# Feed-forward weights summed and rounded in chunks during the attention loop, and a feed-forward block two tiles deep

## The chip, the cores and the metric

The kernel runs on one core of one Trainium2 chip. The time is that of one execution on the device in microseconds (us), the median of several runs. PE is TensorE, DVE VectorE, ACT ScalarE, POOL GpSimd, SP SyncE, whose queue issues all DMAs here.

## What is computed

Two gated residual blocks over x (32 batches of 100 rows, 512 wide) and a context (32 batches of 361 rows, 256 wide):

```
xn = layernorm(x)
q = rmsnorm(xn @ Wq) * gq ; k = rmsnorm(ctx @ Wk) * gk ; v = ctx @ Wv     (16 heads of 128)
x = x + tanh(g_xattn) * (softmax(q k^T / sqrt(128)) @ v) @ Wo

weight_quant(w): s = max(mean(|w|), 1e-5);  clip(round(w / s), -1, 1) * s
act_quant(x):    r = 127 / max(|x| of the row);  round(x * r) / r
bitlinear(x, w) = act_quant(x) @ weight_quant(w)^T
h = layernorm(x)
x = x + tanh(g_ffn) * bitlinear(silu(bitlinear(h, Wgate)) * bitlinear(h, Wup), Wdown)
```

Wgate and Wup are 2048x512, Wdown is 512x2048. Before the products each of the three becomes a matrix of -1, 0 and 1 and one scale, which needs the mean over the whole matrix first.

## The kernel before

**Two blocks, one after the other.** `attention_block` writes x after attention to DRAM (`x1_rows`), 3200 rows. `ffn_block` reads them back in 25 tiles of 128 rows. All DMAs of the first are done before the second begins.

**Attention.** The 32 batches are handled as 16 pairs (`PAIRS`). A pair has 8 units (`UNITS`), a unit being one batch and one group of 4 heads; units are written in twos (`two_turns(i, u, last, par)` with u = 1, 3, 5, 7 and v = u + 1). Matrix factors in fp32 are split into a high and a low bf16 part and multiplied with three matmuls (`product`, lines 23 to 25). Within a unit PE makes keys for unit u+2 (three tiles of up to 128 context rows), scores for unit u+1, and mixes of probabilities and context for unit u. Keys pass through the other engines in a chain: ACT squares them (L554), DVE sums the squares (`sum_keys`, L737), POOL turns the sum into a scale with two small operations (`key_scale`, L986 and L989), DVE scales (`scale_keys`, L747, writes `khat`), ACT takes the high half (L549), POOL the low half (`keys_lo`, L995, a subtract of two 128x512 inputs), and SP turns both with a DMA transpose. POOL also computes the query scale (`query_scale`, L1001) from `qvar` (DVE, L821) and splits the next pair's context into `nat` (`split_ctx`, L1025 and L1027). On DVE `row_max` (L755), `row_bias` (L765, writes `nbias`) and `probs_lo` (L777) serve the softmax.

Every engine has its own in-order list, written out by hand; semaphores tie them together. Two key banks alternate (`keys_ps`), so the keys of tile n wait for `khat` of tile n-2; two shared banks (`shared_ps`) go round queries, squares, mixes and head outputs, and each use waits until DVE has freed the use before last (`shared_free`). Fourteen pairs run in a hardware loop of 7 turns (`BODY` = 2 pairs a turn, `LOOPS` = 7), the last two are written out.

**Feed-forward.** The block loads the three weight matrices (4 MB each) into SBUF, sums absolute values on ACT (`abs_sums`, L1341, four pieces of 128x2048 a matrix), adds over partitions with a matmul (L1266), divides, clips and rounds on DVE (`ternary`, L1477 and L1479), turns every 128x128 piece on PE (L1280) and casts it on ACT (L1353). Only then does the first `gate_up` start. Per tile:

- DVE: statistics (`x_stats`, L1396 and L1399), `x_quant` (L1404 to L1418), `hidden` (L1426 and L1429, four pieces of 512), `hidden_quant` with a pass over 128x2048 (L1441), `residual` (L1448).
- POOL: `deviation`, two small operations (L1243, L1245).
- PE: `gate_up`, 32 matmuls of 512 columns (L1300), the turning of x (L1290), `down`, 16 matmuls (L1308).
- ACT: four Silu (L1367), casts of x (L1358) and of the hidden row (L1373).
- SP: a DMA transpose of the hidden row (L1198), loads and stores.

In step t PE does `gate_up(t + 1)`, turns x of t + 2, and does `down(t)`.

Of the kernel before, what the change touches and what calls it, by code (L numbers as in the profile page):

```python
# [10 lines left out]
EPS = 1e-5  # L11
# [16 lines left out]
def attention_block(nc, x, ctx, g_xattn, wq, wk, wv, wo, gq, gk, x1):  # L28
# [25 lines left out]
    LOOPS = (PAIRS - 1) // BODY  # L54
# [60 lines left out]

    def head(i, u, h):
        return i * (UNITS * G) + (u * G + h)
# [10 lines left out]
    with ExitStack() as stack:  # L128
# [7 lines left out]
        wk_hi, wk_lo = sb("wk_hi", [P, CC, INNER], BF16), sb("wk_lo", [P, CC, INNER], BF16)  # L136
        wq_hi, wq_lo = sb("wq_hi", [P, CM, INNER], BF16), sb("wq_lo", [P, CM, INNER], BF16)
# [28 lines left out]
        yT = sb("yT", [P, NT, QT], F32)  # L166
        xres = sb("xres", [SQ, 2, DM], F32)

# [44 lines left out]
        y_turned, y_added = sem("y_turned"), sem("y_added")  # L213

# [23 lines left out]
        def _(sp):  # L238
# [70 lines left out]
            def turn(i, u, last, par):  # L309
# [15 lines left out]
                if has_scores(u, last):  # L325
                    turn_probs(i, u + 1, 0), turn_probs(i, u + 1, 1)
                if u == UNITS:
# [6 lines left out]

            with sp.Fori(0, LOOPS) as j:
                for r in range(BODY):
                    for u in range(1, UNITS + 1):
                        turn(j * BODY + r, u, False, r)
            for i in range(LOOPS * BODY, PAIRS):
                for u in range(1, UNITS + 1):  # L340
                    turn(i, u, i == PAIRS - 1, i % BODY)
            for b in range(2):
                sp.wait_ge(x1_out[b], PAIRS * 16)
# [3 lines left out]
        def _(eng):  # L347
# [125 lines left out]
            def two_turns(i, u, last, par):  # L473
# [61 lines left out]
            with eng.Fori(0, LOOPS) as j:  # L535
                for r in range(BODY):
                    for u in range(1, UNITS, 2):
                        two_turns(j * BODY + r, u, False, r)
            for i in range(LOOPS * BODY, PAIRS):
# [5 lines left out]
        def _(eng):  # L545
# [66 lines left out]

            def first_turn(i, u):
# [8 lines left out]
            def two_turns(i, u, last, par):  # L622
# [54 lines left out]
                if kv:  # L677
                    keys_hi(i, v + 2, 2)
                if sv:
# [9 lines left out]

            eng.wait_ge(small_in, 48)  # L690
# [25 lines left out]
            with eng.Fori(0, LOOPS) as j:  # L716
                for r in range(BODY):
                    for u in range(1, UNITS, 2):
                        two_turns(j * BODY + r, u, False, r)
            for i in range(LOOPS * BODY, PAIRS):  # L720
# [5 lines left out]
        def _(eng):  # L726
# [115 lines left out]

            def first_turn(i, u):
# [12 lines left out]
            def two_turns(i, u, last, par):  # L856
# [9 lines left out]
                if qu:  # L866
                    queries_lo(i, u, 0)
                if ku:
# [62 lines left out]
                if v == UNITS:  # L931
                    residual(i, 0), residual(i, 1)


            eng.sem_inc(y_added, 1)
            x_stats(-1, 0), x_stats(-1, 1)
# [31 lines left out]
            with eng.Fori(0, LOOPS) as j:  # L968
                for r in range(BODY):
                    for u in range(1, UNITS, 2):  # L970
                        two_turns(j * BODY + r, u, False, r)
            for i in range(LOOPS * BODY, PAIRS):
# [5 lines left out]
        def _(eng):  # L978
# [50 lines left out]

            def first_turn(i, u):  # L1030
# [3 lines left out]
            def two_turns(i, u, last, par):  # L1034
# [25 lines left out]
                if kv:  # L1060
                    keys_lo(i, v + 2, 1), keys_lo(i, v + 2, 2)
                if new_ctx:
                    split_ctx(i + 1, b, 2, 1 - par, ctx_raw)

            pool.memset(ident[:, :], 0.0).then_inc(ident_zero, 1)
# [457 lines left out]
```

## Time and profile before

| what | us |
|---|---|
| median of 3 runs | 2481.73 |
| lowest and highest | 2481.36, 2483.34 |
| the profiled execution | 2482.65 |
| its span | 2480.5 |
| busy in the span: PE, DVE, ACT, POOL | 2256.4, 1903.3, 1577.8, 1200.9 |
| last write of attention's rows issued | 2091.2 |
| first gate/up matmul of the feed-forward block | 2174.4 |

The profile is that of one execution. Its span runs from the first to the last instruction; the execution's own time is 2.15 us longer. Times in rows are us from the span's start, unless marked ns. A matmul row shows the time until its result is there; since matmuls overlap, the distance from one start to the next is what one costs.

### The profile page before, as it was taken

The numbers are of one execution on the slowest core, as the hardware profiler recorded it, in microseconds if no ns is written. First come the engines' busy times: TensorE is split into PE (matmuls) and PEld (weight loads), VectorE is DVE, ScalarE is ACT, GpSimd is POOL, SyncE is SP. The second block draws the span as 40 slices with busy tenths as digits, with TensorE's granted clock in tenths as the row PEclk, the third lists the DMA queues.
The fourth block names the chain that finished last, engine by engine and source line by source line (L and its number), as shares of the span: only waits on it lengthen the run. The fifth ranks groups of instructions, "written<-read, shape, count | busy, mean of one in ns | idle before, by whom it ended". The sixth has DMA issues, their size and how long they took to land. (4 is left out here: it accounts for less than half of the span.)

```text
span 2480.5 us, 52473 instructions
## 1 busy us (share of the span) xinstructions
PE 2256.4 (91%) x16482; PEld 1597.2 (64%) x16634; DVE 1903.3 (77%) x4175; ACT 1577.8 (64%) x3226; POOL 1200.9 (48%) x1538
## 2 busy tenths in 40 slices
PE   2599999999999999999999999999999995589998
PEld 1377777777677767677767777777777773344443
DVE  4588878877878787877787788778887773589996
ACT  3567666766666666666666676667676763744443
POOL 4365646565656565656565656565656551000000
PEclk8799999999999999999999999999999998799999
DMA  6466666666666656666666666666666653434443
GB/s 199 103 112 113 122 111 119 113 121 112 116 116 121 107 118 116 122 112 116 114 122 113 116 112 123 113 115 113 124 113 118 115 113 106 160 77 106 118 114 93
DMA packets 887466, 289.31 MB, mean 117 GB/s; under 512 B 847760, under 2 KB 859312, under 8 KB 886704
## 3 DMA queue, kind: packets, MB, share of 16 engines
q1 hardware_dynamic: 887216, 286.15, 60.0%
q8 instruction: 136, 2.23, 0.4%
q14 instruction: 114, 0.93, 0.2%
HBM read 63.21 MB, written 13.11 MB: 31 GB/s over the span
## 5 line engine op out<-in xcount | busy, mean ns | idle before, releaser
L747 DVE TENSOR_TENSOR khat<-keys_ps,krs 128x512 f32<-128x512 f32 (+1 forms) x384 | 263.4, 686 | 289.9 <-POOL krs L989 289.9
L995 POOL TENSOR_TENSOR ksplit<-khat,ksplit 128x512 bf16<-128x512 f32 (+1 forms) x384 | 444.0, 1158 | 59.8 <-ACT ksplit L549 59.1
L986 POOL TENSOR_SCALAR kvar<-kss 128x4 f32<-128x4 f32 (+1 forms) x384 | 86.2, 225 | 674.0 <-DVE kss L737 674.0
L989 POOL TENSOR_TENSOR krs<-kvar,minus_half 128x4 f32<-128x4 f32 (+1 forms) x384 | 387.0, 1008 | 32.0
L569 ACT ACTIVATE early<-score_ps,nbias,qrs 100x361 f32<-100x361 f32 x512 | 330.5, 651 | 91.0 <-DVE nbias L765 88.5
L578 ACT ACTIVATE psplit<-early,rden 100x361 bf16<-100x361 f32 x512 | 304.9, 596 | 83.0 <-DVE rden L771 81.5
L554 ACT ACTIVATE ksq<-keys_ps 128x512 f32<-128x512 f32 (+1 forms) x384 | 228.6, 596 | 202.4 <-PE keys_ps L25 201.1
L777 DVE SCALAR_TENSOR_TENSOR psplit<-early,rden,psplit 100x361 bf16<-100x361 f32 x512 | 323.1, 641 | 7.8 <-ACT psplit L578 3.7
L549 ACT ACTIVATE ksplit<-khat 128x512 bf16<-128x512 f32 (+1 forms) x384 | 240.2, 625 | 115.5 <-DVE khat L747 105.0
L23 PE MATMUL keys_ps<-wk_hi,ctxT 128*128 128x512 bf16 (+1 forms) x649 | 249.8, 385 | 62.0 <-DVE khat L747 40.6
L755 DVE TENSOR_REDUCE nmax<-score_ps 100x1 f32<-100x361 f32 x512 | 269.1, 526 | 45.9 <-PE score_ps L25 45.9
L24 PE MATMUL keys_ps<-wk_lo,ctxT 128*128 128x512 bf16 (+1 forms) x768 | 293.6, 382 | 6.6 <-issue 0.2
L25 PE MATMUL keys_ps<-wk_hi,ctxT 128*128 128x512 bf16 (+1 forms) x761 | 290.8, 382 | 0.0
L737 DVE TENSOR_REDUCE kss<-ksq 128x4 f32<-128x512 f32 (+1 forms) x384 | 260.0, 677 | 37.9 <-ACT ksq L554 34.9
L23 PE MATMUL shared_ps<-pT,nat 128*128 128x400 bf16 (+1 forms) x768 | 257.0, 335 | 6.5 <-DMA pT<-psplit 5.3
L23 PE MATMUL shared_ps<-xT_hi,wq_hi 128*128 128x200 bf16 x1024 | 256.0, 250 | 1.0 <-DVE uT L731 1.0
L25 PE MATMUL shared_ps<-pT,nat 128*128 128x400 bf16 (+1 forms) x768 | 256.0, 333 | 0.0
L24 PE MATMUL shared_ps<-xT_lo,wq_hi 128*128 128x200 bf16 x1024 | 255.9, 250 | 0.0
L25 PE MATMUL shared_ps<-xT_hi,wq_lo 128*128 128x200 bf16 x1024 | 255.9, 250 | 0.0
L24 PE MATMUL shared_ps<-pT,nat 128*128 128x400 bf16 (+1 forms) x768 | 255.7, 333 | 0.0
L23 PE MATMUL y_ps<-oT_hi,wo_hi 128*128 128x200 bf16 x1024 | 255.0, 249 | 0.5 <-DVE oT_lo L731 0.5
L24 PE MATMUL y_ps<-oT_lo,wo_hi 128*128 128x200 bf16 x1024 | 255.0, 249 | 0.0
(155 smaller groups left out, 5295.6 us busy)
## 6 DMA issues: line engine op xcount, KB each, us to landing
ctx_raw<-in_ctx SPq DMA_DIRECT2D x31, 256.0 KB, 3.0
xin<-in_x SPq DMA_DIRECT2D x32, 200.0 KB
xres<-in_x SPq DMA_DIRECT2D x32, 200.0 KB
x_rows<-xres SPq DMA_DIRECT2D x32, 200.0 KB
xin<-x_rows SPq DMA_DIRECT2D x25, 256.0 KB, 2.8
xres<-x_rows SPq DMA_DIRECT2D x25, 256.0 KB, 2.6
out<-xres SPq DMA_DIRECT2D x25, 256.0 KB, 2.9
kT<-ksplit SPq DMA_TRANSPOSE x384, 3.1
```

The lines of the kernel that those rows point to most:

```text
L23: pe.matmul(out, w_hi, m_hi, start=first, stop=False)
L24: pe.matmul(out, w_hi, m_lo, start=False, stop=False)
L25: return pe.matmul(out, w_lo, m_hi, start=False, stop=last)
L549: return act.activation(out, in_, ACT.Copy)
L569: act.activation(prob[:, b, h, :], score_ps[h % 2][0:SQ, 0:SK], ACT.Exp, bias=nbias[:, b, h:h + 1], scale=qrs[:, v // 2 % 2, r:r + 1], acc ...
L578: act.activation(psplit[0:SQ, h // TWO, 0, h % TWO, 0:SK], prob[:, b, h, :], ACT.Copy, scale=rden[:, b, h:h + 1]).then_inc(p_hi_done, 1)
L737: dve.tensor_reduce(kss[0:KV[t], k, :], ksq[0:KV[t], k, :].rearrange("p (h d) -> p h d", h=G), AX_X, ALU.add).then_inc(kss_done, 1)
L747: dve.tensor_tensor(khat[0:KV[t], k, :].rearrange("p (h d) -> p h d", h=G), keys_ps[k][0:KV[t], :].rearrange("p (h d) -> p h d", h=G), rs, ...
L755: dve.tensor_reduce(nmax[:, b, h:h + 1], score_ps[h % 2][0:SQ, 0:SK], AX_X, ALU.max, negate=True).then_inc(nmax_done, 1)
L777: dve.scalar_tensor_tensor(out=psplit[0:SQ, h // TWO, 1, h % TWO, 0:SK], in0=prob[:, b, h, :], scalar=rden[:, b, h:h + 1], in1=psplit[0:SQ ...
L989: pool.tensor_tensor(krs[0:KV[t], k, :], kvar[0:KV[t], k, :], minus_half[0:KV[t], 0:G], ALU.pow).then_inc(krs_done, 1)
L995: pool.tensor_tensor(ksplit[0:KV[t], t, 1, :], khat[0:KV[t], (u + t) % 2, :], ksplit[0:KV[t], t, 0, :], ALU.subtract).then_inc(k_lo_done, 1)
```

## The change

- The host lays the three feed-forward weights out transposed in one array `w_ffn` of 3 x 128 rows and 8192 columns. The work on them moves into the attention loop, in chunks of 128 rows by 512 columns, one chunk a unit, 16 chunks a loop turn (one matrix a turn).
- Pairs 0 and 1 are written out. Three loop turns (pairs 2 to 7) carry the sums: SP loads a chunk into `w_raw`, ACT takes absolute values and adds them (`sum_chunk`); at the end of a turn DVE adds the 16 partial sums (`weight_sum`) and SP stores them to `w_sums`. Three more turns (pairs 8 to 13) carry the rounding: SP loads the chunk again, POOL makes three passes over it (`round_chunk`), SP stores the bf16 result to `w_tern`. At the start of such a turn DVE computes the matrix's scale (`weight_scale`) from a row that SP loads. Pairs 14 and 15 are written out as before.
- In the last pair SP loads the finished weights into the buffers of Wq and Wk as these come free (`load_ternary`). `yT` shares the buffer of `qsq`.
- The feed-forward block has no weight preparation any more. x is cast on ACT and turned by a DMA transpose instead of on PE. Quantising of the hidden row moves from DVE to ACT, in two halves, each with its own transpose. PE runs `gate_up(t + 2)` ahead of `down(t)`; statistics and `x_quant` are done four tiles ahead.

```diff
+            def load_chunk(j, i, u, k, job):
+                if job == "sum":
+                    sp.wait_ge(w_summed, chunk(i, u) + 1)
+                else:
+                    sp.wait_ge(w_rounded, tern_chunk(i, u) + 1)
+                sp.dma_start(w_raw[:, :], w_ffn[w_rows(j, job), k * CHUNK:(k + 1) * CHUNK]).then_inc(w_raw_in, 16)
+                if job == "tern" and k == 0:
+                    m = j - TERN_LOOPS[0]
+                    sp.wait_ge(w_inv_done, m + 1)
+                    sp.dma_start(w_part[:, :], w_sums[bass.ds(m, 1), :].partition_broadcast(P)).then_inc(w_part_in, 16)
+            def store_chunk(j, i, u, k, job):
+                if job == "tern":
+                    sp.wait_ge(w_rounded, tern_chunk(i, u) + 2)
+                    sp.dma_start(w_tern[w_rows(j, job), k * CHUNK:(k + 1) * CHUNK], w_out[:, :]).then_inc(w_tern_out, 16)
+                elif k == CHUNKS - 1:
+                    sp.wait_ge(w_abs_read, m + 2)
+                    sp.dma_start(w_sums[bass.ds(m, 1), :].rearrange("a p -> p a"), w_abs1[:, :]).then_inc(w_sums_out, 16)
+            def load_ternary(u):
+                for m, part, parts in {4: ((0, 0, 4),), 5: ((0, 1, 4),), 6: ((0, 2, 4), (0, 3, 4), (1, 0, 4)),
+                                       7: ((1, 1, 4), (1, 2, 4), (1, 3, 4)), 8: ((2, 0, 2), (2, 1, 2))}.get(u, ()):
...
             def turn(i, u, last, par, j=None, job=None):          # SP: load_chunk first, store_chunk after turn_probs
...
+            def sum_chunk(j, i, u, k):                            # ACT
+                eng.wait_ge(w_raw_in, (chunk(i, u) + 1) * 16)
+                act.activation(w_raw[:, :], w_raw[:, :], ACT.Abs, accum_out=w_abs[:, k:k + 1]).then_inc(w_summed, 1)
...
                 mixed_hi(i, u, 1)                                 # ACT, odd unit
                 if su:
                     softmax_exp(i, u + 1, 2), softmax_exp(i, u + 1, 3)
+                if job == "sum":
+                    sum_chunk(j, i, u, par * UNITS + u - 1)
...
                     keys_hi(i, v + 2, 2)                          # ACT, even unit
+                if job == "sum":
+                    sum_chunk(j, i, v, par * UNITS + v - 1)
...
+            def weight_scale(j):                                  # DVE, behind queries_lo(i, u, 0), u == 1
+                eng.wait_ge(w_part_in, m * 16 + 16)
+                dve.tensor_reduce(w_tot[:, :], w_part[:, :], AX_X, ALU.add).then_inc(w_tot_done, 1)
...
+            def round_chunk(j, i, u, k):                          # POOL
+                eng.wait_ge(w_raw_in, (chunk(i, u) + 1) * 16)
+                pool.tensor_scalar(w_raw[:, :], w_raw[:, :], w_inv[:, 0:1], ROUND, ALU.mult, ALU.add).then_inc(w_scaled, 1)
+                eng.wait_ge(w_scaled, n + 1)
+                pool.tensor_scalar(w_raw[:, :], w_raw[:, :], ROUND + 1.0, ROUND - 1.0, ALU.min, ALU.max).then_inc(w_clipped, 1)
+                eng.wait_ge(w_tern_out, n * 16 + 16)
+                eng.wait_ge(w_clipped, n + 1)
+                pool.tensor_scalar(w_out[:, :], w_raw[:, :], -ROUND, 1.0, ALU.add, ALU.mult).then_inc(w_rounded, 1)
...
                     key_scale(i, u + 2, 2), keys_lo(i, u + 2, 1), keys_lo(i, u + 2, 2)     # POOL, odd unit
+                if job == "tern":
+                    round_chunk(j, i, u, par * UNITS + u - 1)
                 if new_ctx:
                     split_ctx(i + 1, b, 0, 1 - par, ctx_raw)
                 if kv:
                     key_scale(i, v + 2, 0)
...
                     keys_lo(i, v + 2, 1), keys_lo(i, v + 2, 2)                             # POOL, even unit
+                if job == "tern":
+                    round_chunk(j, i, v, par * UNITS + v - 1)
...
             def step(t, s, ahead):                                # feed-forward, PE
+                if ahead >= 2:
+                    gate_up(t + 2, s)
                 down(t, s)
...
             def step(t, s, ahead):                                # ACT: quantise and cast_hidden are halves of 1024
+                gated(t + 2, s, 0), quantise(t + 1, 1 - s, 0), gated(t + 2, s, 1), cast_hidden(t + 1, 1 - s, 0)
+                cast_x(t + 3, 1 - s), gated(t + 2, s, 2), quantise(t + 1, 1 - s, 1), gated(t + 2, s, 3)
+                cast_hidden(t + 1, 1 - s, 1)
...
             def step(t, s, ahead):                                # DVE
+                x_stats(t + 4, s), down_scale(t, s), hidden(t + 2, s), hidden_scale(t + 2, s)
+                x_quant(t + 4, s), residual(t, s)
...
             def step(t, s, ahead):                                # SP
+                load_x(t + 5, 1 - s), turn_hidden(t + 1, 1 - s, 0), turn_x(t + 3, 1 - s)
+                load_residual(t + 1, 1 - s), turn_hidden(t + 1, 1 - s, 1)   # then the store of t
```

## Rows read from the trace of the kernel before

**Rows 1.** Windows: busy us (count) by engine, granted clock, DMA share, GB/s.

```profile
100.00:2000.00 1900.00, 1832.45 (x14244) 1364.90 (x14365) 1501.52 (x3417) 1307.12 (x2838) 1109.63 (x1401) 0.99 0.65 116
...
2200.00:2250.00 50.00, 46.83 (x219) 21.62 (x223) 46.40 (x97) 22.13 (x27) 3.12 (x8) 1.00 0.47 115
```

**Rows 2.** Waits, 100 to 2060 us: who waited, total us, times, longest.

```profile
PE keys_ps L23 <- DVE khat L747: 23.7, 24, 4.0
...
PE keys_ps L23 <- issue: 14.0, 6, 2.5
```

**Rows 3.** Timeline of POOL, one pair: start, duration, instruction, [idle before].

```profile
1125.01 1.16 POOL L995 TENSOR_TENSOR ksplit<-khat,ksplit 105x512 bf16<-105x512 f32 x1 [0.34 <-ACT ksplit L549]
...
1128.44 0.48 POOL L986 TENSOR_SCALAR kvar<-kss 128x4 f32<-128x4 f32 x1
...
1218.21 1.16 POOL L995 TENSOR_TENSOR ksplit<-khat,ksplit 105x512 bf16<-105x512 f32 x1 [0.34 <-ACT ksplit L549]
1221.29 0.36 POOL L986 TENSOR_SCALAR kvar<-kss 128x4 f32<-128x4 f32 x1 [1.92 <-DVE kss L737]
...
1232.21 1.16 POOL L995 TENSOR_TENSOR ksplit<-khat,ksplit 105x512 bf16<-105x512 f32 x1 [0.34 <-ACT ksplit L549]
1239.79 0.19 POOL L986 TENSOR_SCALAR kvar<-kss 128x4 f32<-128x4 f32 x1 [6.42 <-DVE kss L737]
```

**Rows 4.** Groups of POOL instructions by shape, 300 to 2060 us: total busy, mean ns.

```profile
L1025 POOL CAST nat<-ctx_raw 128x256 bf16<-128x256 f32 x52 | 20.7, 398 | 15.1 <-PE shared_ps L25 15.1
```

**Rows 5.** Timeline of DVE, unit 7 of that pair.

```profile
1218.31 1.08 DVE L765 TENSOR_TENSOR nbias<-nmax,qrs 100x1 f32<-100x1 f32 x1
...
1222.78 0.69 DVE L747 TENSOR_TENSOR khat<-keys_ps,krs 128x512 f32<-128x512 f32 x1 [0.54 <-POOL krs L989]
1223.39 0.15 DVE L821 TENSOR_SCALAR qvar<-shared_ps 100x8 f32<-100x8 f32 x1
```

**Rows 6.** Timeline of PE, same unit.

```profile
1223.87 0.25 PE L23 MATMUL shared_ps<-uT,wv_hi 128*128 128x200 bf16 x1
```

**Rows 7.** Timeline of SyncE's queue, start of that pair.

```profile
1117.26 1.29 SPq L263 DMA_DIRECT2D xres<-in_x  x2
```

**Rows 8.** Groups of ACT instructions by shape, 2060 us to the end.

```profile
L1341 ACT ACTIVATE hid<-g_raw 128x2048 f32<-128x2048 f32 x4 | 7.6, 1900 | 8.4 <-DMA g_raw<-in_L_ffn_w_gate 8.4
```

**Rows 9.** Timeline of SyncE's queue, start of the feed-forward block.

```profile
2094.97 0.38 SPq L1190 DMA_DIRECT2D gate<-in_g_ffn  x1
```

**Rows 10.** Timeline of PE, same stretch.

```profile
2174.41 0.81 PE L1300 MATMUL gate_ps<-gT,xqT 128*128 128x512 bf16 x3 [1.04 <-ACT xqT L1358]
```

**Rows 11.** Timeline of DVE, the first tile's statistics to its quantised row.

```profile
2184.83 0.69 DVE L1396 BATCH_NORM_STATS2 st<-xin 128x6 f32<-128x512 f32 x1
...
2188.74 0.49 DVE L1418 TENSOR_SCALAR xq<-xin,xinv 128x512 f32<-128x512 f32 x1
```

**Rows 12.** The page's DMA issues: count, KB each, median us from issue to landing.

```profile
xin<-x_rows SPq DMA_DIRECT2D x25, 256.0 KB, 2.8
...
kT<-ksplit SPq DMA_TRANSPOSE x384, 3.1
```

**Rows 13.** Timeline of DVE, steady feed-forward tile.

```profile
2341.78 0.75 DVE L1426 SCALAR_TENSOR_TENSOR hid<-up_ps,gus,sil 128x512 f32<-128x512 f32 x1
...
2348.00 1.29 DVE L1441 TENSOR_SCALAR hid<-hid,hinv 128x2048 f32<-128x2048 f32 x1
...
2353.51 0.74 DVE L1426 SCALAR_TENSOR_TENSOR hid<-up_ps,gus,sil 128x512 f32<-128x512 f32 x1
```

**Rows 14.** Timeline of PE, same stretch.

```profile
2345.62 3.62 PE L1308 MATMUL down_ps<-dT,hT 128*128 128x512 bf16 x16
2349.07 1.03 PE L1300 MATMUL gate_ps<-gT,xqT 128*128 128x512 bf16 x4
```

**Rows 15.** Timeline of PE, the last tile.

```profile
2460.98 3.62 PE L1308 MATMUL down_ps<-dT,hT 128*128 128x512 bf16 x16
2471.00 4.42 PE L1308 MATMUL down_ps<-dT,hT 128*128 128x512 bf16 x10 [6.41 <-DMA hT<-hq]
```

More of the change, by code:

```diff
@@ L114, in unit, with chunk, tern_chunk @@
         return i * UNITS + u
+    def chunk(i, u):
+        return i * UNITS + (u - 1) - SUM_LOOPS[0] * CHUNKS
+    def tern_chunk(i, u):
+        return i * UNITS + (u - 1) - TERN_LOOPS[0] * CHUNKS
     def head(i, u, h):
@@ L310, in turn @@
+            def turn(i, u, last, par, j=None, job=None):
+                if job is not None:
+                    load_chunk(j, i, u, par * UNITS + u - 1, job)
                 if not last and u == 1:
@@ L534, in _ @@
             first_turn(-1, UNITS)
[L535 to L539, printed above, removed]
+            for i in range(SUM_LOOPS[0] * BODY):
+                for u in range(1, UNITS, 2):
+                    two_turns(i, u, False, i % BODY)
+            for loops, job in ((SUM_LOOPS, "sum"), (TERN_LOOPS, "tern")):
+                with eng.Fori(*loops) as j:
+                    for r in range(BODY):
+                        for u in range(1, UNITS, 2):
+                            two_turns(j * BODY + r, u, False, r, j, job)
+            for i in range(TERN_LOOPS[1] * BODY, PAIRS):
                 for u in range(1, UNITS, 2):
@@ L715, in _ @@
             first_turn(-1, UNITS)
[L716 to L720, printed above, removed]
+            for i in range(SUM_LOOPS[0] * BODY):
+                for u in range(1, UNITS, 2):
+                    two_turns(i, u, False, i % BODY)
+            for loops, job in ((SUM_LOOPS, "sum"), (TERN_LOOPS, "tern")):
+                with eng.Fori(*loops) as j:
+                    for r in range(BODY):
+                        for u in range(1, UNITS, 2):
+                            two_turns(j * BODY + r, u, False, r, j, job)
+            for i in range(TERN_LOOPS[1] * BODY, PAIRS):
                 for u in range(1, UNITS, 2):
@@ L867, in two_turns @@
                     queries_lo(i, u, 0)
+                if u == 1 and par == 0 and job == "tern":
+                    weight_scale(j)
                 if ku:
@@ L967, in _ @@
             first_turn(-1, UNITS)
[L968 to L972, printed above, removed]
+            for i in range(SUM_LOOPS[0] * BODY):
+                for u in range(1, UNITS, 2):
+                    two_turns(i, u, False, i % BODY)
+            for loops, job in ((SUM_LOOPS, "sum"), (TERN_LOOPS, "tern")):
+                with eng.Fori(*loops) as j:
+                    for r in range(BODY):
+                        for u in range(1, UNITS, 2):
+                            two_turns(j * BODY + r, u, False, r, j, job)
+            for i in range(TERN_LOOPS[1] * BODY, PAIRS):
                 for u in range(1, UNITS, 2):
@@ L1245, in deviation, with step @@
                 pool.tensor_tensor(rstd[:, :], var[:, :], minus_half[:, :], ALU.pow).then_inc(rstd_done, 1)
-            def step(t, s, ahead1, ahead2):
-                if ahead2 and not (isinstance(t, int) and t + 3 >= TILES):
-                    deviation(t + 3)
-            deviation(0), deviation(1), deviation(2)
+            def step(t, s, ahead):
+                if ahead >= 4:
+                    deviation(t + 4)
+            for t in range(4):
+                deviation(t)
             steps(eng, step)
@@ L1387, in _ @@
+            cast_x(0, 0)
+            eng.wait_ge(xqT_in[0], 16)
+            cast_x(1, 1)
+            for f in range(FC):
+                gated(0, 0, f)
+            gated(1, 1, 0)
+            quantise(0, 0, 0)
+            gated(1, 1, 1)
+            cast_hidden(0, 0, 0)
+            cast_x(2, 0)
+            gated(1, 1, 2)
+            quantise(0, 0, 1)
+            gated(1, 1, 3)
+            cast_hidden(0, 0, 1)
             steps(eng, step)
```

460 lines of the change are left out of this document (255 added, 205 removed).

## The prediction

> **What bounds the kernel now.** I read the windows first, to cut the span into stages. In the attention loop PE is busy 1832 of 1900 us at a granted clock of 0.99; in the feed-forward stage DVE and PE are both near 93% [rows 1]. The reader is to see that a mean over the whole span hides two different limits and, between them, a stretch in which neither works.
>
> The waits come next. In 1960 us of attention PE waits 23.7 us for khat (DVE) and 14.0 us in six waits named "issue", one at each jump back of the seven-turn loop, so 2.3 us each [rows 2]. Nothing else holds it for long: attention is bound by PE's own stream, and whatever makes PE wait there is lost in full. The other engines have room only between the points where PE needs them.
>
> Then the timelines. The feed-forward block issues its first DMA at 2094.97 [rows 9] and its first real matmul starts at 2174.41 [rows 10]: 79.4 us in which weights are loaded, summed, rounded and turned. After that one tile takes 11.7 us (2341.78 to 2353.51), set by DVE, which works without a gap [rows 13]; PE needs less: down takes 3.45 us (2345.62 to 2349.07) for 16 matmuls of 512 columns, 0.216 each, so 48 of them are 10.35 us [rows 14].
>
> **The change, part by part.** The sum is made in the profiled execution: 2482.65 us, of which the span is 2480.5. The median of the runs shown, 2481.73, lies 0.9 below it.
>
> *Start of the feed-forward block.* Summing, rounding and turning of weights go. What is late next is the first tile's own chain: load issued at 2095.0, landing 2.8 later [rows 12]; statistics, POOL's deviation and quantising 4.4 (2184.83 to 2189.23) [rows 11]; a cast like the 128x512 pieces elsewhere, 0.6 (my estimate from 1.9 us for 128x2048 [rows 8], by columns plus a fixed part); a DMA transpose 3.1, as for kT [rows 12]; handing over 0.1. That is 11.0, so PE starts at 2106.0: **-68.4**. The load of the sums lands in the shadow of the row's load.
>
> *From the first matmul to the end of the last gate/up.* Before: 2174.4 to 2461.0 [rows 10, 15], 286.6 us. DVE loses the 1.29 us quantising of the hidden row (0.1 of it overlapped) [rows 13], and its wait of some 0.3 for POOL's deviation, which is now a tile further ahead: 11.7 - 1.5 = 10.2. PE's x transposes go, leaving 10.35. PE becomes the bound by a hair; I take 10.4. ACT gets the two quantising halves: with four Silu, four pieces of 1024 columns at about 1.0 and one cast it has some 7 us of work per tile, and a whole tile of slack towards PE. After: two gate/up ahead of the loop (13.8), 2.8 because PE starts cold (after 6.4 us idle ten matmuls take 0.44 each, twice the 0.22 [rows 14, 15]; I let that last as long as 26 matmuls would need at full rate, 5.6 us, my estimate, half of it lost), 2.5 waiting for the third tile's row, which stands behind hidden(0) on DVE and a half hidden row on SyncE, then 22 steps of 10.4 and a last gate/up of 6.9: 254.8. **-31.8.**
>
> *Tail.* Before, 19.5 us from 2460.98 to the end, with PE idle 6.4 and then cold [rows 15]. Now two downs are left to do while the last hidden row is quantised and turned in halves: 2.3 until its scale, 4.2 on ACT, 3.1 for the transpose, 1.7 for eight matmuls, 3.5 for residual and store: 14.8. **-4.7.**
>
> *Loops.* Seven turns become two loops of three and two pairs written out: four jumps back instead of six, 2 x 2.3: **-4.7** [rows 2].
>
> *Sums, 48 chunks on ACT.* By 1.9 us for 2048 columns [rows 8] a chunk is 0.55 and 0.1 to read the accumulator. ACT has 593 us of room in 1900 [rows 1] and idles 0.5 to 0.9 for DVE right behind both places. DVE's needs are met within 0.1. I take **+2**, between 0 and 48 x 0.65 = 31.
>
> *Rounding, 48 chunks on POOL.* Nothing in the trace is a POOL tensor_scalar of 128x512. The nearest rows are the cast of 128x256, 0.40 [rows 4], and the two-input subtract of 128x512, 1.16 [rows 3]. A tiny POOL operation is 0.19 [rows 3], so the cast doubled is 0.61; I take 0.65 and 0.1 for each wait, so 2.25 a chunk; bounds 1.5 and 3.8. Behind the chunk POOL holds key_scale of the next unit, for which DVE's scale_keys waits, and behind that qvar, for which PE waits. The gap it has to fit in is, in units 5 and 7, 1.92 us; in unit 1, 1126.17 to 1128.44 less 1.1 of split_ctx, 1.2; in unit 3 about the same; in even units 5 to 6.4 [rows 3]. So POOL is late by 0.3 twice and 1.05 twice a pair. Slack at PE: qvar ends at 1223.54, the matmul that needs its bank starts at 1223.87 [rows 5, 6]: 0.33.
>
> There is a second cost. At 1218.31 an nbias on 100 single elements took 1.08 us, where a qvar of 100x8 took 0.15; it ended at 1219.39, with the POOL subtract of 1218.21 that ended at 1219.37 [rows 3, 5]. A DVE operation with two inputs in SBUF can be held until a POOL one is done. Beside each chunk stand two or three such operations (probs_lo, nbias), so DVE or POOL may lose up to 1.0 more per chunk. With it all, odd units cost PE 1.0, 1.0, 1.7, 1.7 = 5.4 a pair; without it 1.4. I take 3.6 and 0.4 for the even ones, whose gap swallows the chunk but not all of DVE's holding: 4.0 x 6 pairs = **+24**. Ends: 0, and with 3.8 us a chunk (1.55 more on each odd unit) 6 x (5.4 + 6.2 + 0.8) = 74.
>
> The Trainium skill, SBUF — State Buffer, "Who interferes with whom", says that a DVE instruction with two SBUF inputs contends with a GpSimd instruction that reads SBUF, one waiting for the whole of the other. The nbias row agrees (1.08 us). By it alone the rounding would be 6 x 5.8, or 35 us. The GPSIMD Engine Reference of the same skill, "Elementwise — side-by-side cycle accounting", gives about 1.03 cycles an element for bodies of up to two operations; an estimate by it is 0.44 us of streaming a pass, near the 0.42 of the doubled cast.
>
> *Scales, three times.* weight_scale makes DVE wait for a row that SyncE loads only behind the xres loads of 1117.26 to 1118.55 and the chunk [rows 7]; landing 2.8 later, about 1122, and four small operations, where DVE would have gone on at about 1120. Queued behind it are scale_keys and the second query half. 2 us a time: **+6**, between 0 and 9.
>
> *Last pair.* 6.3 MB of ternary weights are loaded; the last 3.5 MB are issued behind the last probability transpose, some 20 us ahead of the block's end, so hidden. Transposes queued behind earlier parts: **+1**, between 0 and 8. The yT that shares qsq adds no wait: PE has read the one before it writes what the other holds.
>
> Sum: -68.4 - 31.8 - 4.7 - 4.7 + 2 + 24 + 6 + 1 = -76.6, so 2406.0 for the profiled execution and **2405 us** as a median.
>
> **The rivals.**
> *A. The chunks are hidden.* POOL runs with 0.55 a pass and DVE's holding falls in its own waits. For it: POOL is busy only 58% of the loop [rows 1]. Against: the 1.92 and 1.2 gaps. Then the attention costs are some 5: 2482.65 - 109.6 + 5 = 2378, as a median 2377.
> *B. POOL is slow.* A pass is as dear as the two-input subtract, 1.16. The rounding is 74 instead of 24: 2405 + 50 = 2455.
> *C. Feed-forward keeps DVE's pace.* If quantising on ACT and the transposes through SyncE return as waits and a tile still takes 11.7, 22 x 1.3 = 29 are not gained: 2434. For it: DVE's list is only 0.15 shorter than PE's. Against: each result is due a tile later.
> *D. Slower than before.* The three passes sit in POOL's in-order queue ahead of key_scale, and each lateness reaches PE through scale_keys. To eat the 100 us that is left without the rounding, the 24 odd chunks must cost 4.2 each where 2.25 us a chunk makes it 1.35 with all holding: 2.85 us more a chunk, so passes from about 1.6 us on. At 2.3 a pass (7.2 a chunk) odd chunks cost 6.3 and even ones, now longer than their gap, 1: 175 instead of 24, 2556. Against: the 0.40 cast.
>
> **How the numbers follow.** Forecast (2392 to 2420) 0.55; A 0.16; B, with all between it and the forecast, 0.17; C 0.09; D 0.03. The range takes A, C and half of B: 2376 to 2442. A measurement of this kernel tells no change within 0.2%, 5 us. Faster by more: all but D, 0.96; within: 0.01; slower: 0.03.
>
> **What would show it.** Right: first gate_ps matmul some 11 us behind the block's first DMA; 10.4 us a tile with PE without gaps; three POOL tensor_scalar of 0.65 in each unit of pairs 8 to 13; pairs 2 to 7 as long as before within 0.5 us; pairs 8 to 13 longer by 4 and, in every second, 2 more, with PE's waits before shared_ps named to DVE's qvar; nbias and probs_lo longer beside POOL's passes. Wrong: a pass far from 0.65, sum pairs that grow, a tile above 11 us, or PE waiting for DMA in the loop.

## The result, and the profile after

The changed kernel takes **2459.65 us** (median of 4 runs, 2458.04 to 2462.24); the kernel before, run beside it, 2482.53. The ratio is 0.9909 [0.9895, 0.9923]: 23 us faster, where 77 were forecast. 2459.65 lies above the range of 2376 to 2442. The profiled span is 2460.4 us.

Two cuts settle where the difference lies. The first is the feed-forward block. SyncE's queue at its border and PE's matmuls (start, duration, what, idle before):

```profile
2171.67 0.97 SPq L292 DMA_DIRECT2D x_rows<-xres  x2
2175.58 0.84 SPq L1355 DMA_DIRECT2D xin<-x_rows  x2
```

```profile
2186.85 1.89 PE L1443 MATMUL gate_ps<-wq_split,xqT 128*128 128x512 bf16 x4 [15.56 <-DMA xqT<-xqb]
...
2299.24 3.62 PE L1452 MATMUL down_ps<-wk_split,hT 128*128 128x512 bf16 x16
2309.60 3.62 PE L1452 MATMUL down_ps<-wk_split,hT 128*128 128x512 bf16 x16
...
2444.28 3.62 PE L1452 MATMUL down_ps<-wk_split,hT 128*128 128x512 bf16 x16
```

The first matmul starts 11.3 us behind the first DMA (11.0 forecast), a tile takes 10.36 (10.4), it is 257.4 from the first matmul to the end of gate/up (254.8), and the rest takes 16.1 (14.8). The rows [rows 9, 10, 13, 15] are what these were forecast from. From the last store of attention to the end the block takes 288.7 us where it took 389.3: 100.6 gained, 104.9 forecast.

So attention takes the rest: its last store is at 2171.67 instead of 2091.16, **80.5 us later**, of which 28 were forecast. The windows, cut at those stores, tell which pairs (one pair a row: length, PE, PEld, DVE, ACT and POOL busy, granted clock of PE, DMA share, GB/s). Pairs 4 to 10:

```profile
616.00:749.00 133.00, 122.64 (x947) 90.76 (x945) 98.20 (x225) 89.66 (x203) 72.61 (x92) 0.96 0.67 123
749.00:875.00 126.00, 120.05 (x942) 88.52 (x940) 98.05 (x225) 89.23 (x202) 72.89 (x92) 1.00 0.74 133
875.00:1010.00 135.00, 124.12 (x961) 91.95 (x960) 98.50 (x225) 90.28 (x203) 72.66 (x93) 0.96 0.70 123
1010.00:1135.00 125.00, 122.29 (x955) 91.14 (x953) 98.36 (x225) 89.54 (x202) 73.23 (x94) 0.99 0.73 133
1135.00:1278.00 143.00, 127.87 (x956) 92.90 (x955) 100.95 (x227) 86.59 (x187) 90.98 (x117) 0.93 0.66 122
1278.00:1407.00 129.00, 120.00 (x920) 88.52 (x918) 98.78 (x223) 84.83 (x185) 89.80 (x115) 0.97 0.73 137
1407.00:1546.00 139.00, 129.31 (x978) 93.90 (x976) 101.42 (x228) 87.42 (x188) 91.69 (x118) 0.95 0.66 128
```

In the kernel before all pairs from 1 to 14 take 122 to 127. Here the second pairs of the rounding turns (9 below; 11 and 13 alike) take 128 to 129, which is the rounding as forecast; the sum pairs 2, 3, 5 and 7 take 124.6 to 125.7, within the same band, so the sums on ACT cost little if anything. But every pair that begins a turn behind a turn with chunks (4, 6, 8, 10, 12) is 9 to 18 us too long. Not the work in a pair, but something at its beginning.

The waits of 100 to 2060 us (who waited, for what: total, times, longest) name it, since most of these are few and their longest are long:

```profile
DVE khat L858 <- POOL krs L1128: 310.1, 243, 8.5
...
PE keys_ps L23 <- DVE khat L858: 35.8, 26, 9.6
PE shared_ps L23 <- DVE qvar L932: 25.1, 18, 7.5
DVE w_tot L965 <- DMA w_part<-w_sums: 24.4, 3, 11.7
POOL nat L1164 <- DMA ctx_raw<-in_ctx: 20.4, 3, 8.9
...
PE keys_ps L23 <- issue: 10.5, 4, 2.8
```

PE names DVE, DVE names POOL, but POOL and DVE themselves wait for DMAs, so the next view is the queue that issues them. SyncE's queue at the turn into pair 4, one with a store of sums ahead of it:

```profile
613.80 1.68 SPq L362 DMA_DIRECT2D w_sums<-w_abs  x1
615.58 0.74 SPq L292 DMA_DIRECT2D x_rows<-xres  x2
626.76 0.71 SPq L288 DMA_DIRECT2D xres<-in_x  x2
631.78 0.36 SPq L345 DMA_DIRECT2D w_raw<-in_ffn  x1
632.48 0.40 SPq L271 DMA_DIRECT2D ctx_raw<-in_ctx  x1
```

and its queue in the middle of a turn (pair 8 to 9) and at a jump back (9 to 10):

```profile
1281.01 1.15 SPq L288 DMA_DIRECT2D xres<-in_x  x2
1282.51 0.37 SPq L345 DMA_DIRECT2D w_raw<-in_ffn  x1
...
1410.51 1.56 SPq L288 DMA_DIRECT2D xres<-in_x  x2
1415.61 0.35 SPq L345 DMA_DIRECT2D w_raw<-in_ffn  x1
1416.29 0.35 SPq L350 DMA_DIRECT2D w_part<-w_sums  x1
```

Three things are to be seen. The store of sums, 128 pieces of 4 bytes (half a kilobyte), stands ahead of the stores of x rows, and SyncE, which waits for these before it may overwrite xres, goes on 10.4 us later (2.0 at the end of pair 8). Between xres and w_raw lies 0.35 us in mid-turn, but 3.5 at the jump back from pair 9 to 10 and 4.3 at the one into pair 4. And the row for the scale stands behind all of it. What it does to PE (timelines of POOL and PE, pair 4):

```profile
636.32 0.40 POOL L1164 CAST nat<-ctx_raw 128x256 bf16<-128x256 f32 x1 [8.88 <-DMA ctx_raw<-in_ctx]
```

```profile
639.57 0.35 PE L23 MATMUL shared_ps<-uT,wv_hi 128*128 128x200 bf16 x1 [7.46 <-DVE qvar L932]
```

and in pair 10 (DVE, then the windows around PE's stall):

```profile
1419.68 0.28 DVE L965 TENSOR_REDUCE w_tot<-w_part 128x1 f32<-128x128 f32 x1 [6.14 <-DMA w_part<-w_sums]
```

```profile
1410.00:1420.00 10.00, 6.71 (x50) 4.64 (x48) 3.40 (x9) 4.31 (x10) 2.50 (x4) 1.00 0.43 122
1420.00:1430.00 10.00, 7.93 (x21) 2.92 (x22) 7.21 (x18) 5.32 (x12) 7.07 (x11) 0.50 0.66 128
1430.00:1440.00 10.00, 10.00 (x98) 8.93 (x97) 7.49 (x18) 6.12 (x13) 7.76 (x11) 0.99 0.59 123
```

After a wait of 4.0 us PE's granted clock is 0.50 for about 10 us, the lower of its two levels (1.2 of 2.4 GHz), and then full again. Ten us at half clock lose some 5 us of PE's work, so this stall of 4 us costs about 9.

### The profile page after: what moved, and what is told of

The parts are those of the page before. It is cut to its first block and busy times, and to the rows that moved or that the text cites. A ratio compares the mean times of both kernels' runs of the same rounds, so it can differ in the third digit from the quotient of the medians.

```text
span 2460.4 us, 52723 instructions
## 1 busy us (share of the span) xinstructions
PE 2247.8 (91%) x16336; PEld 1575.7 (64%) x16336; DVE 1851.5 (75%) x4149; ACT 1598.7 (65%) x3326; POOL 1303.7 (53%) x1679
## 5 line engine op out<-in xcount | busy, mean ns | idle before, releaser
L1125 POOL TENSOR_SCALAR kvar<-kss 128x4 f32<-128x4 f32 (+1 forms) x384 | 80.2, 209 | 616.7 <-DVE kss L848 614.7
L23 PE MATMUL keys_ps<-wk_split,ctxT 128*128 128x512 bf16 (+1 forms) x768 | 301.1, 392 | 68.6 <-DVE khat L858 51.4
L888 DVE SCALAR_TENSOR_TENSOR psplit<-early,rden,psplit 100x361 bf16<-100x361 f32 x512 | 337.2, 668 | 8.8 <-ACT psplit L672 3.7
L643 ACT ACTIVATE ksplit<-khat 128x512 bf16<-128x512 f32 (+1 forms) x384 | 241.1, 628 | 145.4 <-DVE khat L858 123.8
L24 PE MATMUL keys_ps<-wk_split,ctxT 128*128 128x512 bf16 (+1 forms) x768 | 299.0, 389 | 0.0
L25 PE MATMUL keys_ps<-wk_split,ctxT 128*128 128x512 bf16 (+1 forms) x768 | 298.3, 388 | 0.0
L23 PE MATMUL shared_ps<-xT_hi,wq_split 128*128 128x200 bf16 x1024 | 257.0, 251 | 1.5 <-DVE uT L842 1.3
L24 PE MATMUL shared_ps<-xT_lo,wq_split 128*128 128x200 bf16 x1024 | 257.0, 251 | 0.0
L25 PE MATMUL shared_ps<-xT_hi,wq_split 128*128 128x200 bf16 x1024 | 256.8, 251 | 0.0
```

Source lines behind the costliest of these rows:

```text
L23: pe.matmul(out, w_hi, m_hi, start=first, stop=False)
L24: pe.matmul(out, w_hi, m_lo, start=False, stop=False)
L25: return pe.matmul(out, w_lo, m_hi, start=False, stop=last)
L643: return act.activation(out, in_, ACT.Copy)
L888: dve.scalar_tensor_tensor(out=psplit[0:SQ, h // TWO, 1, h % TWO, 0:SK], in0=prob[:, b, h, :], scalar=rden[:, b, h:h + 1], in1=psplit[0:SQ ...
```

## The experiments

The theory (Q): the 52 us that were not forecast are made at the turns, in SyncE's queue. Its main rivals: POOL's passes (P), the new loops (S). Each time below is a median, measured beside the kernel before on the same chip, and followed by its ratio to that kernel. The chips differ a little, so distances to the changed kernel are given by ratios, that is 0.9909 less the ratio, times 2482, unless medians are named. Lengths of single pairs are from the profiled execution of each kernel. Where an edit changes what the kernel computes, the text says what it leaves out.

**No chunks at all.** Loops by `for loops, job in ((SUM_LOOPS, None), (TERN_LOOPS, None))` on every engine, the ternary weights filled with zeros once from ACT's queue.

> Left out: the whole work in chunks (its loads, sums, rounding passes, stores and the scale); the ternary weights are zeros, written once while the weights of attention are split. Both loops of three and the new feed-forward block stay. Theory Q (the unforeseen time comes from what the chunk work puts into SyncE's queue around a loop turn, made larger by PE's half clock behind each stall): every pair is back to the 124.4 us of before on average, attention ends at about 2087 (two jumps fewer), the whole takes about 2378. Rival S (the two loops and the written-out pairs themselves cost, or the new feed-forward block changes attention): pairs 4, 6, 8, 10, 12 stay over 130 us and the whole takes 2400 or more.

2384.29 us, 0.9587 [0.9571, 0.9603]. From the first store of x rows to the last, attention takes 1849.5 us, before 1848.2, changed 1929.1. So the chunk work costs all of the 80. S is out, but the total is 6 above Q's 2378: the loops don't give the 4.7 of the two missing jumps, since pairs 4, 6, 10 and 12 take 128. SyncE's row of such a turn shows a likely reason:

```profile
624.09 1.13 SPq L288 DMA_DIRECT2D xres<-in_x  x2
629.11 0.41 SPq L271 DMA_DIRECT2D ctx_raw<-in_ctx  x1
```

3.9 us across SyncE's own jump back, where the kernel before has 0.8 (372.43 to 373.19; its row of the same place):

```profile
370.55 1.88 SPq L263 DMA_DIRECT2D xres<-in_x  x2
373.19 0.40 SPq L246 DMA_DIRECT2D ctx_raw<-in_ctx  x1
```

**xres later.**
```diff
 SP, turn(), u == UNITS:
-                        for b in range(2):
-                            sp.wait_ge(x1_out[b], i * 16 + 16)
-                            load_x(i + 1, b, xres, xres_in)
 SP, turn(), behind turn_probs:
+                if u == 2 and started(i):
+                    for b in range(2):
+                        sp.wait_ge(x1_out[b], i * 16)
+                        load_x(i, b, xres, xres_in)
```

> The wait for the stored rows and the load of xres go from the end of a pair to SyncE's unit 2 of the next pair; all else as in the changed kernel. Theory Q: pairs 4 and 6 lose their 9 us, pairs 8, 10 and 12 lose at least half of the 10 to 12 us that they take beyond a steady rounding pair, the whole takes 2415 to 2430. Rival R (the 4-byte store holds the transfers behind it, whoever waits for it): pairs 4, 6 and 8 stay as they are, only some 5 us go. Rival P (POOL's passes and what they hold on DVE make the long pairs): no more than 10 us go, and only in pairs 4 and 6.

2440.49 us, 0.9822 [0.9806, 0.9838]: 21.6 less. Pairs 4, 6, 8, 10, 12 lose 2 to 3.5 each, where Q wanted 9 and half of the rest. The rest is spread over pairs without a turn, and differences of 2 us between single pairs of two runs mean nothing here. None of the three expectations came true: more went than R's 5 and P's 10, and Q's sizes did not come. The wait is part of it, but the stall stays.

**No store of sums.** `sp.sem_inc(w_sums_out, 16)` in place of L362's DMA.

> Left out: the three stores of the partial sums in pieces of 4 bytes (a semaphore is raised in their place; the sums in DRAM are taken once from other data at the start, so the scale is another number). Theory Q: pairs 4 and 6 fall back to about 125 us and pair 8 loses some 8, while pairs 10 and 12, ahead of which no such store stands, stay: about -24, so 2435. Rival P: pairs 4 and 6 improve, pair 8 doesn't: -16. Rival J (the jump back itself and what waits behind it): nothing changes in any pair, 2459.

2433.03 us, 0.9788 [0.9772, 0.9804]: 30 less, by medians 27. Pairs 4 and 6 fall to 128.1 and 126.4, as without any chunks (128.3, 127.6); pair 8 loses 6.3; 10 and 12 stay at 141. As Q said. Pairs 2 to 7, which still load and sum their chunks here, take 748.3 us together, and without any chunk work 749.9: the sums on ACT and their loads are free.

**One pass.** L1177 and L1180 left out.

> Two of POOL's three passes over a chunk are left out (the third reads the raw chunk and scales it, so the weights are not ternary); all loads, stores and waits stay. Theory Q: the steady cost of rounding, about 5 us a pair, falls to near 0, so about -25, and the 10 to 12 us more of pairs 8, 10 and 12 stay: about 2433. Rival P: the long first pairs of a turn go as well, since POOL's lateness makes them: about -50, 2408.

2428.05 us, 0.9767 [0.9751, 0.9783], 35 less. Pairs 9, 11, 13 fall from 129.0, 127.9, 128.0 to 123.8, 122.8, 121.5; the first pairs of a turn keep their length beyond that (137.5, 136.8, 135.9). P is out for the long pairs; the steady rounding costs 5 to 6.5 a pair.

**Scale row early.** It is loaded half a turn ahead, and for the first matrix between the two loops:
```diff
-                    sp.wait_ge(w_inv_done, m + 1)
-                    sp.dma_start(w_part[:, :], w_sums[bass.ds(m, 1), :].partition_broadcast(P))
+                if job == "tern" and par == BODY - 1 and u == 4:
+                    sp.wait_ge(w_tot_done, j - TERN_LOOPS[0] + 1)
+                    load_sums(bass.ds(j - TERN_LOOPS[0] + 1, 1))
```

> The row of partial sums for the next matrix's scale is loaded half a turn earlier (unit 4 of the turn's second pair; for the first matrix between the loops, without waiting for the last store of sums), so DVE finds it there; all else as in the changed kernel. Theory Q (what is left of the long pairs 8, 10 and 12 is DVE's wait for this row, doubled by PE's half clock behind it): each of the three falls by about 8, so about -25, 2435. Rival C (the late context row and the late first chunk hold POOL and so the same PE instruction): PE waits for khat just as long, under 5 us go, 2455.

2449.73 us, 0.9869 [0.9848, 0.989]: 10 less, 5.5 and 5.8 in pairs 10 and 12 but 1.3 in pair 8, whose row still stands behind the last store. Less than the 25 of Q: C has its share too: PE still waits for khat up to 8.2 us (9.6 before the move) and for qvar up to 8.8.

**Three moves together.** xres later, scale row early, and the store of sums issued by ACT (`act.dma_start(...)` at chunk 0 of the next turn, the last one between the loops).

> Three moves together: xres waits and loads in unit 2 of the next pair; the partial sums are stored from ACT's DMA queue one turn later (and the last between the loops) instead of from SyncE's; the row for the scale is loaded early. Theory Q: pairs 2 to 7 as long as without chunks (123 to 128), pairs 8, 10 and 12 at about 131 and 9, 11, 13 at 128: 20 us of -24 for the store, -25 for the row and -10 for xres remain after their overlap, about -55, so 2405. Rival T (a stall at the turn stays whatever is moved, because SyncE's jump takes 3 us): 2425 or more. If ACT's queue doesn't spare the others the store, pairs 4 and 6 stay at 134.

2429.82 us, 0.9792 [0.9766, 0.9817]. By its total this is T's number and not Q's 2405, and it is no better than leaving out the store alone, though two more moves are in it. Pair 4 is at 128.6, but pair 6 at 133.3 and pair 8 at 138.5. DVE at the start of pair 8, ACT in pair 6:

```profile
1132.76 0.29 DVE L976 TENSOR_REDUCE w_tot<-w_part 128x1 f32<-128x128 f32 x1 [5.42 <-DMA w_part<-w_sums]
```

```profile
891.16 0.63 ACT L646 ACTIVATE ksplit<-khat 128x512 bf16<-128x512 f32 x1 [7.90 <-DMA kT<-ksplit]
```

and the DMAs issued around pair 8's start (KB each, us to landing):

```profile
ctx_raw<-in_ctx SPq DMA_DIRECT2D x1, 256.0 KB, 10.0
ctx_raw<-in_ctx SPq DMA_DIRECT2D x1, 105.0 KB, 12.3
...
w_part<-w_sums SPq DMA_DIRECT2D x1, 64.0 KB, 10.5
```

SyncE's transfers land 10 to 12 us after their issue instead of 3, with the half kilobyte issued at 1120.6 on another engine's queue just ahead of them. At the three other places where ACT issues such a store (378.0, 627.4 and about 879.4 us, beside transposes and not beside loads), the first transpose of probabilities behind it lands after 7.6, 10.9 and 10.7 us, where the kernel without these stores has 5.0, 3.6 and 3.5. But only pairs 6 and 8 are longer for it; a late transfer costs only where something waits for it. The move to ACT moved the stall. T is taken up with the sums on the chip below. The Trainium skill (DMA: Bandwidth & Descriptors, "Issuing engines are not separate DMA queues") says that DMAs of all engines run on the same 16 DMA engines and interleave; the trace agrees.

**What makes that store slow.** Four stores of 128 pieces in pair 1, otherwise the kernel without stores of sums:
```diff
+                if isinstance(i, int) and i == 1 and u in (2, 4, 5, 6):
+                    wide = {2: 1, 4: 16, 5: 1, 6: 128}[u]
+                    sp.dma_start(scratch[u], ident[:, 0:wide]).then_inc(w_fill, 16)   # u == 5: rows 512 bytes apart
```

> The kernel without the stores of sums, and in pair 1, where nothing else is added, four stores of 128 pieces from SBUF: in unit 2 pieces of 4 bytes side by side in DRAM, in unit 4 pieces of 64 bytes, in unit 5 pieces of 4 bytes that lie 512 bytes apart, in unit 6 pieces of 512 bytes. Theory Q (it is the small piece): 4 bytes land after about 8 us or more in both forms and the transposes behind them are late; 64 and 512 bytes land within 3. Rival N (writers of neighbouring 4 bytes get in each other's way): 8 side by side, 3 apart. Rival V (any store of 128 pieces into a busy queue takes this long): all four take 8.

One execution (2441.28 us). The DMAs around the first, third and fourth by issue, then the second (`near`: 4 bytes side by side, `far`: 4 bytes 512 apart, `by`: 64 and 512 bytes):

```profile
ctx_raw<-in_ctx SPq DMA_DIRECT2D x1, 256.0 KB, 11.2
ctx_raw<-in_ctx SPq DMA_DIRECT2D x1, 105.0 KB, 12.4
...
near<-ident SPq DMA_DIRECT2D x1, 0.5 KB, 13.5
```

```profile
far<-ident SPq DMA_DIRECT2D x1, 0.5 KB, 2.2
```

```profile
by<-ident SPq DMA_DIRECT2D x1, 64.0 KB, 2.9
```

```profile
by<-ident SPq DMA_DIRECT2D x1, 8.0 KB, 2.2
```

Of the three expectations this is N's: the same 128 pieces of 4 bytes land after 2.2 us when they lie apart in DRAM and after 13.5 when they lie side by side, and the loads issued behind them land 11 to 12 us after their issue. So it is not the size of a piece. The two stores stand at different places, though: `near` has 361 KB of loads behind it, `far` has transposes around it. Two other runs speak against the place as the cause. Without `near`, the same two loads in the same unit land after 3.3 and 2.6 us (kernel without stores of sums), so their traffic alone is not slow. And the neighbouring words that ACT stores in the kernel with three moves stand (at three of four places) among transposes and delay these to 7.6 us and more, while the transposes around `far` land after 3.2 to 4.4. Each form was timed once, and the two were not swapped; why neighbours cost this was not tried.

**Sums kept on the chip.** PE adds them over the partitions; nothing goes through DRAM. xres later.
```diff
+                if job == "tern" and u == 1 and par == 0:                  # PE, behind queries(i, u, 0)
+                    eng.wait_ge(y_added, i * 2 + 1)
+                    eng.wait_ge(w_abs_read, MATRICES + 1)
+                    pe.matmul(y_ps[0][:, 400:403], ones[:, 0:1].broadcast_to([P, P]), w_abs3[:, :],
+                              start=True, stop=True).then_inc(w_part_in, 1)
```

> The partial sums never go to DRAM: they stay in SBUF, one TensorE matmul of 128x3 against ones adds them over the partitions at the start of each rounding turn, DVE makes the scale from PSUM; xres waits and loads in unit 2 of the next pair. Chunks as in the changed kernel. Theory Q (what was left in the kernel with three moves, pair 6 at 133 and pair 8 at 138.5, is the 4-byte store, which slows all transfers of its time whatever queue it stands in): pairs 4 and 6 at 128, pair 8 at 129, pairs 10 and 12 at 132, so 14 less than that kernel, about 2415. Rival T (those two long pairs come from something else at the turn): 2430.

2411.04 us, 0.9711 [0.9669, 0.9753]: 49 below the changed kernel, and T's 2430 is out. Pairs 4 and 6 at 126.5 and 126.4, pair 8 at 130.9, 10 and 12 at 132.8 and 132.2. The same with the wait for the stored rows back at the pair's end:

> The kernel with the partial sums kept on the chip and chunks in all units (2411 us), but the wait for the stored rows and the loads of xres back at the end of a pair, as in the changed kernel. Theory Q (that wait is dear only where the 4-byte store stands ahead of it): SyncE waits 2.5 to 4.2 there, as in the kernel before, and little changes, 2411 to 2417. Rival X (the wait at a turn costs by itself, ahead of the 3 us jump): the 20 us that its move gave in the changed kernel come back, 2425 or more.

2423.45 us, 0.9753 [0.9725, 0.9781]: between the two expectations. SyncE waits 2.75 at most at a turn, and still the kernel is 12 us dearer by medians, 10 by ratios; the two intervals overlap slightly, so this part is the less certain one. Of the 49, some 39 by ratios are then the way of the sums through DRAM (the stores and the load of the row, 30 and 10 when tried one by one) and some 10 the wait at a turn.

**Where the rounding's 5 us a pair are.** First come memsets in place of the passes in the changed kernel, so nothing is rounded. Then come wide chunks in even units only, once on the kernel with three moves and once on the one with sums on the chip.
```diff
-                pool.tensor_scalar(w_raw[:, :], w_raw[:, :], w_inv[:, 0:1], ROUND, ALU.mult, ALU.add).then_inc(w_scaled, 1)
+                pool.memset(w_raw[:, :], 1.0).then_inc(w_scaled, 1)        # and so for the other two
```

> The three passes of POOL over a chunk are replaced by three memsets of the same buffers, which read nothing; no rounding is done. All loads, stores and waits stay. Rival H: if the memsets take about as long as the passes, the 5 us a pair go nevertheless (pairs 9, 11, 13 at 123), about -30, 2430, and nbias and probs_lo are no longer stretched. Theory L: what goes is in proportion to the time POOL is spared; at 0.65 each little, 2455.

2438.37 us, 0.9813 [0.9796, 0.983], 24 less. Pairs 9, 11, 13: 123.5, 124.6, 123.1, so the 5 us go. But a memset took 0.525 us where the passes of the changed kernel took 0.97, 0.675 and 0.65:

```profile
L1177 POOL TENSOR_SCALAR w_raw<-w_raw,w_inv 128x512 f32<-128x512 f32 x48 | 46.7, 972 | 4.8
L1180 POOL TENSOR_SCALAR w_raw<-w_raw 128x512 f32<-128x512 f32 x48 | 32.4, 675 | 9.1 <-POOL w_raw L1177 9.1
L1186 POOL TENSOR_SCALAR w_out<-w_raw 128x512 bf16<-128x512 f32 x48 | 31.1, 649 | 9.3 <-POOL w_raw L1180 9.3
```

A memset chunk with its waits takes 1.9, just the gap of 1.92 in units 5 and 7 [rows 3], a real one 2.7. So this run can't part lateness from holding (POOL late for what PE needs, against DVE and POOL holding each other up). My expectation of a loss in proportion was wrong, since only what exceeds the gap counts.

The rows of the changed kernel say who is held. L1177 took 0.70 in the six chunks in which no probs_lo or nbias of DVE (two inputs in SBUF) was under way at its start, and 0.86 to 1.05 in the 42 in which one was; the memsets, which read nothing, took 0.53 at the most in all 48. In those six the second pass took 0.96 or 0.97 instead, with a probs_lo begun just ahead of it; one of them (POOL and DVE; the row that writes psplit is probs_lo, two of them):

```profile
1270.40 0.70 POOL L1177 TENSOR_SCALAR w_raw<-w_raw,w_inv 128x512 f32<-128x512 f32 x1
1271.21 1.44 DVE L888 SCALAR_TENSOR_TENSOR psplit<-early,rden,psplit 100x361 bf16<-100x361 f32 x2
1271.30 0.96 POOL L1180 TENSOR_SCALAR w_raw<-w_raw 128x512 f32<-128x512 f32 x1 [0.19 <-POOL w_raw L1177]
```

So the 0.3 that the first pass takes above the other two is not its scale per partition but mostly holding, and POOL pays it. DVE pays less: its probs_lo and nbias of pair 9 take 32.3 us together (21.5 and 10.8), and 31.0 without chunks.

Chunks in even units are to part the two:

> As the one with three moves together, and each rounding chunk is 1024 columns wide and goes only into the even units, where POOL had 5 to 6.4 us free; the last pass writes its bf16 in place into the raw chunk. Theory L (the steady 5 us a pair are POOL's lateness for key_scale and the query scale in odd units): pairs 9, 11 and 13 fall from 128 to about 123, so 25 to 30 less than the kernel with three moves, about 2378. Rival H (they come from DVE's operations held while POOL passes over SBUF, wherever that is): the same pass time, so the same 5 a pair, 2405.

2416.64 us, 0.9722 [0.9703, 0.9741], 17 below the same with 512 columns in all units. Pairs 9, 11 and 13 take 126.0 each. DVE's probs_lo got longer (mean 761 ns in pair 9, 683 in the changed kernel, 643 without chunks), so DVE is held more than before and yet less time is lost: that speaks for L for about half of the 5, and what stays has both. It is not shown cleanly, since the wide passes are also shorter for their columns (1.34, 1.09 and 1.11 us for 1024), so that POOL's chunk work falls from some 21 to 16 us a pair; H had the pass time unchanged.

> The same, with rounding chunks of 1024 columns in even units alone. Steady rounding pairs at 126 instead of 128 and the first pairs of a turn at 129 to 130: some 14 below the same kernel with chunks in all units, about 2402, and 55 below the changed kernel. If the gain of even units was the trace's chance, both are alike.

**2394.08 us, 0.9647 [0.9603, 0.9692]**: the fastest that still does the whole work, 86 below the kernel before and 66 below the changed one by medians. It is 17 below the same with chunks in all units, near the 14 expected, and these two intervals too overlap slightly. Its pairs 4, 8, 9 and 10, to be held against those of the changed kernel:

```profile
610.00:738.00 128.00, 124.95 (x957) 92.45 (x956) 97.99 (x224) 90.05 (x203) 72.99 (x92) 0.97 0.71 130
...
1111.00:1239.00 128.00, 125.30 (x971) 93.73 (x969) 102.69 (x229) 86.03 (x187) 87.67 (x104) 0.97 0.71 137
1239.00:1366.00 127.00, 120.16 (x922) 89.15 (x920) 100.83 (x224) 84.30 (x184) 87.75 (x104) 0.97 0.74 140
1366.00:1496.00 130.00, 126.96 (x981) 94.30 (x980) 102.47 (x227) 86.53 (x188) 87.85 (x105) 0.97 0.75 136
```

## Why the prediction was wrong

- *Start of the feed-forward block, first matmul to last gate/up, tail*: 100.6 gained of the 104.9 forecast. Rival C is out: a tile takes 10.36, and from 2216 us to the end of gate/up PE is busy without a gap. Ahead of that it waits twice for DVE's hidden row, 1.5 and 2.9 us, where 2.5 was priced.
- *Rounding, +24*: near in size, and partly by luck. A pair costs 5 instead of 4, so some 30 by the three second pairs; what two of the three passes cost is 35 by the ratio of one_pass. The place was right: POOL is late, mostly in the odd units. The split was not. A chunk takes 2.7 instead of 2.25, so the lateness was priced too low. Holding was priced too high: 0.3 a chunk on POOL (within the 2.7) and 1.3 a pair on DVE, where up to 1.0 a chunk was taken. Two errors of opposite sign left a number near the measured one. Rival B (2455) gives the right total for the wrong reason: its passes of 1.16 and its 74 us are not there.
- **The step that failed is the term "Sums, 48 chunks on ACT", taken at +2.** ACT's part is free, as taken. But the edit issues a DMA as well, the store of the sums, and I gave it no price: 27 to 30 us, for three stores. It stands ahead of the x rows in SyncE's queue, and the transfers issued behind it land late, whichever queue it stands in.
- *Scales, +6*: the place was right, the price too low, and partly for the same cause. The load stands behind the xres loads, as I said; that SyncE's jump adds 3.2 us ahead of it, that the last store of sums lies ahead of the first of these loads, and that PE's clock halves after the wait, I did not have. DVE waits 24.4 us in three waits (11.7, 6.1 and 6.5), where 2 each were taken. Moved early it gives 10, above the upper end of 9; with the sums off DRAM the two together give 39 by ratios.
- *Loops, -4.7*: nothing came (attention without chunks takes 1849.5, before 1848.2). PE does have four waits of 2.6 at jumps instead of six of 2.3, but SyncE's jump, 0.8 us from DMA to DMA before, takes 3.5 to 4.3 now with chunks and 3.9 to 4.2 without. Why it grew was not tried.
- *Last pair, +1*: pair 15 takes 105.6, before 105.9. Right.
- A general fault beside these: each stall was priced at its length. After the stall of 4.0 us in pair 10 PE runs at 0.50 for about 10 us, so it costs about 9.

The terms that failed add up to most of the 55 between forecast and result: 28 for the stores, 4 or more for the scales, 6 for the loops, 6 to 11 for the rounding and 4 for the feed-forward block, less 2 for the sums on ACT and 1 for the last pair, so 45 to 50. The rest is not assigned. The wait for the stored rows at a turn, worth 10 when it is moved in the kernel with the sums on the chip, may be part of it, but the kernel before has the same wait, and it was not moved there. The parts overlap, and their sizes come from kernels that each move other things as well, so this split is good to some 5 us a term.

## What to carry to other kernels

Price each DMA that an edit adds as if it were the slow one, however few bytes it has, and look at what is queued behind it on its engine: here three stores of half a kilobyte cost nearly as much as three passes over 12 MB of weights. Results of one column over the partitions should not go to neighbouring words in DRAM; add them over the partitions with a matmul, as here, or write them apart, which was tried for one store and not in the whole kernel. Where a rare event sits in a loop, read the first body after each turn apart from the mean, since a stall of some us on PE is paid again at half clock (pair 10); and put background work into the gaps that hold it whole.

## What was unexpected of the hardware

- 128 pieces of 4 bytes to neighbouring addresses: 7.7 to 11.0 us to land in the changed kernel, 13.5 in the test; 512 bytes apart 2.2, in one store of each. Transfers issued behind it, on the same queue or another, landed late too: 10.0 to 12.4 us for loads that otherwise take about 3. The Trainium skill (DMA: Bandwidth & Descriptors, "Queues, rings and completion order") says that a completion is posted only behind all earlier writes of its DMA engine, across queues; loads that are late by the time of the slow store fit that, though no run here shows the posting itself.
- SyncE's jump back takes 3.2 to 4 us more than the same place without a jump (3.5 to 4.3 against 0.35), and in the kernel before it took 0.7 to 0.8 in all. The Trainium skill (Advanced Engine Details and Errata, "Control Flow Timing") gives about 0.11 us for a compare and branch; the trace shows that this is not what a turn of a long loop costs.
- A POOL pass over 128x512 fp32 took 0.61 to 0.70 unheld, with constants or with a scale per partition, and up to 1.05 when a DVE operation with two inputs in SBUF was under way at its start; over 128x1024 1.09 to 1.11 with constants (means), and with a scale 1.13 unheld and 1.41 held. A memset of 512 columns took 0.53 in either case. So a POOL operation that only writes was not held, and one that reads was.
